# Spreading the list writes of twelve sequences over four turns of the attention loop

## What is computed

```
x = layernorm(x + attention(x))     # 16 heads of 16 features, softmax over 256 keys
x = layernorm(x + experts(x))       # 8 experts, the best 2 of a token, hidden width 1024

# inside experts(x):
gates = softmax(x @ gating_w);  topk_w, topk_idx = top_k(gates, 2);  norm_w = topk_w / sum(topk_w)
position = running count of the tokens that chose this expert before;  valid = position < 1280
buf[e, position] = x[token];  h = relu(buf @ w1[e] + b1[e]);  out_e = h @ w2[e] + b2[e]
out[token] += out_e[e, position] * norm_w
```

## Time and profile before

| | |
|---|---|
| timed runs, median (lowest to highest), 3 runs | 821.24 us (820.07 to 822.61) |
| profiled execution, span from first to last instruction | 856.8 us; nothing is given around it |
| TensorE busy | 784.5 us, 92% |
| DVE, ACT, POOL busy | 605.1, 442.1, 410.2 us |
| list writes (L533) | 64, 65.5 us of POOL |
| mean granted TensorE clock | 0.971 of full |

### The profile page before, as it was taken

How to read it: one execution, slowest core, us unless ns; L and a number is a source line. 1 busy time by engine, 2 the same in 40 slices (tenths; PEclk the granted TensorE clock), 3 DMA queues, 4 the chain that set the end, 5 groups by cost and what they waited for, 6 DMA issues and landing times.

```text
span 856.8 us, 16628 instructions
## 1 busy us (share of the span) xinstructions
PE 784.5 (92%) x5919; PEld 648.5 (76%) x5919; DVE 605.1 (71%) x1325; ACT 442.1 (52%) x753; POOL 410.2 (48%) x595
## 2 busy tenths in 40 slices
PE   7699989999989985896999999999999999999994
PEld 7577766677667653585889898898898888988993
DVE  5768878888888885683756856756657568665983
ACT  3166757777666664542534534534345345443670
POOL 1011245555555546457146445254364462556675
PEclk9799999999999998799899999999999999999998
DMA  5677765555555572326145245253352451533741
GB/s 158 135 165 161 161 153 113 114 113 114 116 114 110 115 141 73 116 51 180 20 91 109 41 89 115 43 130 50 81 111 40 96 112 31 140 57 57 288 179 46
DMA packets 71534, 92.75 MB, mean 108 GB/s; under 512 B 12972, under 2 KB 55885, under 8 KB 71324
## 3 DMA queue, kind: packets, MB, share of 16 engines
q1 hardware_dynamic: 53308, 67.95, 31.0%
q0 software_dynamic: 16928, 22.15, 14.9%
q10 hardware_dynamic: 1216, 1.57, 0.8%
HBM read 39.18 MB, written 26.89 MB: 77 GB/s over the span
## 4 chain that ended last, share of the span: by engine, by line
PE 69%; DVE 14%; issue 5%; POOL 3%; another core or an unknown queue 3%; DMA 2%; ACT 2%; ACTq 1%; POOLq 0%; DVEq 0%; SPq 0%
PE bank L1718 14%; DVE negm L890 10%; PE wide L1687 8%; PE wide L1685 8%; PE wide L1686 8%; PE bank L985 7%; PE bank L1720 7%; PE wide L1030 5%; PE bank L1664 2%; PE wide L1048 2%; PE bank L1095 2%; PE bank L1064 1%; PE bank L994 1%; POOL slot_list L533 1%
## 5 line engine op out<-in xcount | busy, mean ns | idle before, releaser
L1359 POOL DMA_INDIRECT acc_rows<-o_w,lists x70 | 120.4, 1720 | 181.6 <-ACT o_w L1508 167.9
L890 DVE TENSOR_REDUCE negm<-wide 128x4 f32<-128x1024 f32 x128 | 156.1, 1222 | 50.5 <-PE wide L1030 31.7
L630 ACT ACTIVATE probs<-wide 128x1024 f32<-128x1024 f32 x128 | 131.0, 1024 | 89.1 <-PE wide L1048 68.9
L1475 ACT ACTIVATE h<-wide,b1T 128x512 f32<-128x512 f32 (+1 forms) x200 | 115.0, 600 | 96.8 <-PE wide L1687 69.1
L1720 PE MATMUL bank<-stack,h_lo 128*128 128x256 f32 x560 | 156.9, 280 | 0.0
L1685 PE MATMUL wide<-g_hi,stack 128*128 128x512 f32 (+1 forms) x400 | 140.8, 352 | 5.2 <-DVE g_lo L1536 4.1
L1687 PE MATMUL wide<-g_hi,stack 128*128 128x512 f32 (+1 forms) x400 | 140.1, 350 | 0.1
L1686 PE MATMUL wide<-g_lo,stack 128*128 128x512 f32 (+1 forms) x400 | 140.1, 350 | 0.0
L1508 ACT ACTIVATE o_w<-o_b,lists 128x256 f32<-128x256 f32 x70 | 35.7, 510 | 148.6 <-DVE o_b L1646 135.5
L1718 PE MATMUL bank<-stack,h_hi 128*128 128x512 f32 x304 | 108.7, 401 | 1.3 <-DVE o_b L1646 1.3
L1720 PEld LDWEIGHTS bank<-stack,h_lo 128*128 128x128 f32 x560 | 105.6, 189 | 0.0
(11 more groups left out here) (211 smaller groups left out, 1640.9 us busy)
## 6 DMA issues: line engine op xcount, KB each, us to landing
stack<-qk SPq DMA_DIRECT2D x180, 128.0 KB, 4.2
w_raw<-in_L_ffn_w SPq DMA_DIRECT2D x16, 1024.0 KB
x_sb<-in_L_attn_x SPq DMA_DIRECT2D x16, 256.0 KB, 5.1
x_rows<-x SPq DMA_DIRECT2D x16, 256.0 KB
acc_rows<-x SPq DMA_DIRECT2D x16, 256.0 KB
acc_sb<-acc_rows SPq DMA_DIRECT2D x8, 512.0 KB, 11.1
out<-acc_sb SPq DMA_DIRECT2D x8, 512.0 KB
x_rows<-zrow SPq DMA_DIRECT2D x2, 1152.0 KB, 6.6
```

Source lines behind the costliest of these rows:

```text
L630: nc.scalar.activation(probs[:, i % 4].rearrange("p x c t -> p x (c t)"), shifted_banks(i)[:, :, :], ACT.Exp, scale=SCALE).then_inc(exp_do ...
L890: nc.vector.tensor_reduce(negm[n % 2][:, :, :, u].rearrange("p c x -> p x c"), score_banks(PAIRS * n + u)[:, :, :].rearrange("p x (c t) -> ...
L1359: nc.gpsimd.indirect_dma_start(out=acc_d, out_offset=bass.IndirectOffsetOnAxis(ap=lists[:, e, QC * c + r, 0:1], axis=0), in_=o_w[c][:, r, ...
L1475: ins = nc.scalar.activation(h[u % 2][:, t], banks[BZ[u % 4]][:, t], ACT.Relu, bias=b1T[:, FT * e + f:FT * e + f + 1])
```

## The change

For sequences 0 to 11 the four indirect DMAs are no longer issued at turns 8m + 51 and 8m + 52, two at each, but at 8m + 52, 53, 54 and 55, one at each, in the order (c, k) = (0,0), (0,1), (1,0), (1,1). Each now waits for `exp_done` to reach turn - 23, that is for the exponentials of the turn before. Its waits for `dest_done`, `token_done` and `weight_done` are issued for each write, where they stood once for two. The writes themselves and those of sequences 12 to 15 are the same.

```diff
         ENTRY, WRITE = (48, 45, 45, 44), ((51, 46, 46, 45), (52, 47, 50, 46))
+        SPREAD = 52
...
-            def into_lists(m, c):
+            def into_lists(m, c, ranks=range(TOPK)):
                 if m == 0 and c == 0:
                     pool.wait_ge(filled, 80)
                 pool.wait_ge(dest_done, m + 1)
                 pool.wait_ge(token_done, m + 1)
                 pool.wait_ge(weight_done, m + 1)
-                for k in range(TOPK):
+                for k in ranks:
                     nc.gpsimd.indirect_dma_start(
...
                 m = due(turn, LIST, LTAIL)
                 if m is not None:
                     entries(m)
+                for i, (c, k) in enumerate(itertools.product(range(QC), range(TOPK))):
+                    m = due(turn, SPREAD + i, LTAIL)
+                    if m is not None:
+                        pool.wait_ge(exp_done, turn - ST0)
+                        into_lists(m, c, (k,))
                 for c in range(QC):
                     m = routed(turn, WRITE[c])
-                    if m is not None and m != FIRST:
+                    if m is not None and m >= LTAIL and m != FIRST:
                         into_lists(m, c)
```

## The result

The changed kernel took 823.61 us in the median of 20 runs (820.41 to 825.46), the kernel before 821.0 us (818.54 to 822.8, 20 runs) beside it. The ratio is 1.003, with a 95% interval of 1.002 to 1.004. So it is slower, by some 2.6 us. The forecast was 821.0 and no change. The time lies in its range, but it moved clear of noise, and that is the rival "POOL becomes late in the tail", given 0.09.

What follows compares the result with a forecast made beforehand. TensorE was busy 92% of the profile, with list-write stalls taken to exist only there. Of 18.8 us removed from the profile, 0 was in timed runs: 821.24 - 0 + 0 = 821 us, range 808 to 824.5.

Steps and rivals of the forecast that it cites:

- POOL becomes late in the tail: Rival: behind sequence 11's write 4, POOL's slips pass on; 822 to 824 us, deciding from a 2.5 us slip; chance 0.09.
- The stall: Attention stage, at list-write bursts: TensorE's completions come late, 24.2 us in the profile; 18.8 go there, 0 in timed runs.
- "faster" rival: Attention stage: the stall is real in timed runs and goes; 802 us, or 812 with half gone; chance 0.21.
- a cost of recording: Attention stage: many small instructions make many trace records, whose collection stalls the profile alone; timed runs keep 821 us.
- the span near 838: Sign in the profile after: 856.8 - 18.8 = 838 us, with timed runs unmoved.
- Records are lost exactly here: Attention stage row-maxima: 9 of 128 start without a recorded releaser, read as support for a stall in the profile alone.
- POOL in sequences 0 to 10: Writes 3 and 4 move by about 1 and 2 us; 3.4 us idle cover remains before `xT_hi`; 0 on the path.
- Sequence 12's first two follow, then write 4: POOL, end of attention stage: sequence 11's write 4 waits for turn 142's exponentials; five of the eight remain back to back.
- 0 (POOL's waits covered): Timed-run term for POOL's added waits: at most 0.75 us per sequence, 9 us in all, under idle time.
- SP is passed by nothing: its waits for landed lists stand at turn 147, four turns behind the last moved write.: Queues step, SP's list loads: the moved writes delay nothing there.
- no move: Sequence 11's write 3: its exponentials end at 329.99, just before its slot at 330.15, so it stays.

Runs made afterwards that it cites:

- Place alone, the 2.1-us gap removed: Kernel before, sequence 11's fourth write issued behind sequence 12's first two, six satisfied POOL waits added in each of sequences 0 to 10: ratio 1.0016, 822.38 us.

## Why the prediction failed

**The stall.** The conclusion that the timed runs don't contain it was right: its 15 to 24 us were not there to be won, and the "faster" rival (0.21) was worth nothing. The reason was half wrong. I called it "a cost of recording"; the same kernel recorded again has none of it, with four writes in a row in every sequence and eight at the end but for the wait for DVE (row 316.72 above). Hence "the span near 838" for the kernel after could not come: it was 821.5. The sentence drawn on the Trainium skill (NOTIFIC — the notification-queue block, section 7.1) may or may not describe what happened in that one execution: the missing releasers are in it alone, and no run here shows its cause. "Records are lost exactly here" is not shown either: both profiles hold 16628 instructions, and only releasers are missing. The same section sets holding producers back against losing a record, so the missing releasers do not speak for it as the prediction says. The cause stays open.

**POOL in sequences 0 to 10.** Right by its steps: gaps before the third and fourth writes (1.89, 0.85), 3.14 us left ahead of `xT_hi` where 3.4 were worked out, nothing on the path. The run with these eleven alone is the test (0.9995).

**Sequence 11: the step that failed.** The order was foreseen to the instruction ("Sequence 12's first two follow, then write 4"), and its lateness then priced "0 (POOL's waits covered)". The term was measured at about +2.6 us. Its error is one sentence: "SP is passed by nothing: its waits for landed lists stand at turn 147, four turns behind the last moved write." I compared turns, though the same document says that turns don't tie the engines to each other. SP's wait is not for a turn but for the landing of just this write. On the clock the fourth write goes from 3.96 to 7.89 us behind the first. These 3.9 us are two more writes ahead of it (2 x 1.27), 0.8 of waiting for DVE's entries (an idle time of 1.08 in place of 0.30), and 0.6 because the third write waits for exponentials (0.89 in place of 0.30), where "no move" was foretold from the profile with the stall. The write landed 1.1 us faster than in the kernel before (3.4 in place of 4.5), so the load goes from 8.53 to 11.39, 2.9 us later. POOL's own work covers a part of that, and the first gather goes from 14.04 to 15.75 and 15.06 in two profiles.

**The rival that came.** Its sum was right (822 to 824 us), its mechanism by half. It placed the harm behind write 4 of sequence 11, in the factors of sequence 13, and priced extra waits and a gap of up to a turn. Those factors come only 1.1 us later (from 11.06 to 12.15), under the 2.5 us from which it was to decide. What was late was write 4 itself, its landing, the list load and the gathers; the factors that POOL then delays are those of sequence 14. That the price fitted is partly luck.

**What carries the 2.6 us.** The fourth write's place does, shown by undoing it alone (0.9997) and doubling it (1.0051). None of the kernels in this comparison has the long gap. Place alone, the 2.1-us gap removed, gave 1.0016 (1.0001 to 1.0031), and the change without waits 1.0014 and 1.0026. The three runs with waits and late fourth write gave 1.0026 to 1.003. Up to about 1 us may thus be the waits' share *when* the write is late; the intervals overlap, and that is left open. Open too is which of the two ways behind the gathers, POOL's queue or TensorE's transposes, passes the delay on: the two profiles of the kernel after differ, and no run separates them.

## What to carry to other kernels

When an instruction moves past others of its queue, write down who waits for its *landing*, and compare times on the clock, not positions in a written order. The last item of a series deserves its own sum: eleven of twelve moved groups were free here, the twelfth was the whole result. Before reasoning about a feature of a profile that the timed runs can't contain, take a second profile of the same kernel.

## What the runs showed of the hardware

- One execution of a program was recorded at 856.8 us of span, the same program later at 819.4, with the timed medians 821.24 and 820.79. The 24 us of stalls without a releaser stood in the first alone.
- Three satisfied waits issued a second time on POOL (one instruction more in its record), some 480 us ahead of the place, cost 1.5 us (1.0006 to 1.0032) through some 2.1 us more in which POOL did nothing: gaps of 2.98, 2.83 and 2.86 us in three kernels with 862 recorded POOL instructions, 1.28 in the one with 867, and 0.70 to 0.72 in those with 861, 895, and 926 to 932. One packet of program moves during the gap; that POOL waited for it is inferred. The Trainium skill (Runtime: NRT & Kernel Launch, Instruction fetch mechanics) calls the cost of crossing a boundary between blocks of program mostly hidden; if the inference holds, it is hidden here in most placements, and 2.1 us in one. A comparison of two kernels whose difference is a microsecond should look at this before the edit is blamed.
- An indirect write of 128 entries of 8 bytes took POOL 0.97 to 1.55 us and landed 2.5 to 5.4 us after its start, among the eight writes at the end of the attention stage in the kernel after. Sequence 11's fourth took 3.42 us, the list load behind it 3.55 us: in that profile 7 us lie between the late write and the first gather that can use it.
